# A Mamba and mixture-of-experts block on one core: softplus, D product and gating by quarters, row copies by way of DRAM, and the combine weights in a gate bank

## The chip, the core and the metric

The kernel runs on one core of a Trainium2 chip, as one launch. The metric is the device time of that core in microseconds (us). Engines are named as in the profile: PE is the matrix engine, DVE the vector engine, ACT the scalar (activation) engine, POOL the general engine, SP the queue that issues most DMAs.

## What is computed

Eight sequences of 256 tokens with 256 features pass through three sublayers, each behind a layer norm and a residual: half of a mixture-of-experts FFN, a Mamba mixer with its own MLP, and the same FFN again.

```python
scores = sigmoid(x @ gate_w); topk_w, topk_i = top_k(scores, 6)        # 32 experts
act = silu(x @ wg) * (x @ wu)                                           # 96 wide each
routed = einsum('tef,efd,te->td', act, wd, combine)                     # + shared FFN, 192 wide
# Mamba, 512 channels, 16 states:
z, x, B, C, dt = split(h @ in_proj.T)
dt = softplus(dt @ dt_proj.T + dt_proj_b)
x = silu(causal_conv(x, 4 taps) + conv_b)
h = exp(dt * A) * h + (dt * x) * B           # over 256 time steps, by channel and state
y = sum_n h * C + x * D_param
out = (y * silu(z)) @ out_proj.T
```

## The kernel before

Everything lies with features on partitions and tokens along the free axis. The 512 Mamba channels are four quarters (JC = 4) of 128 partitions. The recurrence of a quarter runs as 8 pairs of states, so there are 32 **units** (UNITS). A unit u is two items: `ub` (PE spreads B into a `side` bank, DVE multiplies it by dt·x, ACT makes the decays) and `unit` (DVE runs the scan over 512 elements, PE spreads C into another `side` bank, DVE multiplies, POOL adds up).

The sequences are software-pipelined over **steps** t = 0 to 9. In step t the first FFN of one sequence, the Mamba mixer of the sequence before it, and the MLP and second FFN of earlier ones run together. Steps 3 to 5 are a hardware loop. In steps 1 and 3 to 7 the two FFN calls share matmuls 512 wide; in steps 2, 8, 9 and 0 they are 256 wide. Mamba is present in steps 1 to 8. Steps 7 and 8 are "own" steps: the second FFN works on the sequence whose MLP ends in the same step, so its routing stands between the MLP and the FFN.

The order of work is planned in Python. `items_of(t)` lists heavy items (MLP chunks `gum`, `down`; FFN chunks `cmb`, `g`, `u`, `down` with the DVE products `by_g`, `by_u` and POOL's `by_comb`) and light items (norms, projections, units, routing `rq`). `merge` spreads the light ones over the heavy ones in proportion to lengths from the tables LENGTH and SHORT. Every engine walks this list in order; DVE and POOL use `late_order`, which holds some items back by a few places.

The projection of a step consists of `split` 0 (B and the dt rank), `split` 1 and 2 (C), `x` 0 and 1 (x with its convolution), `z` 0 and 1, `dt` 0 and 1, `sp` (logarithm on ACT, correction on DVE), `sp_dt` (dt finished), `sp_x` (dt·x), `y0` (x·D). A split writes three bf16 parts into `parts`, which overlays the `decays` buffers; DMAs then copy groups of 32 rows into `bst` and `cst`, and their semaphore is `stacked`. The buffers `ubuf`, `lbuf`, `tmp`, `dtr` and the padded x all overlay `ring`. `yz` multiplies y by silu(z) before the output projection `outp` (L827).

PE has three `gub` banks for `g`, `u` and `gum`, and three `side` banks taken in turn by everything else, `cmb` (L695, the combine weights of three chunks, copied to SBUF by ACT at L862) among them. A bank is waited for through the semaphore of its use three uses ago.

## Time and profile before

| | |
|---|---|
| median of 3 runs | 1869.39 us (1867.44 to 1872.44) |
| the profiled execution | 1871.1 us, its span 1869.3 us |
| PE busy | 1573.3 us (84%) |
| DVE busy | 1300.1 us (70%) |
| POOL, ACT busy | 719.7 us (38%), 696.6 us (37%) |
| mean granted PE clock | 0.940 |

Busy time is the union of an engine's instructions; the rest of the span it is idle. The time of a step is the distance between the FFN ends: about 117, 197, 198, 217, 220, 217, 200, 211, 189 and 99 us for steps 0 to 9.

### The profile page before, as it was taken

To read this page: it belongs to the slowest core of one execution; us is meant where nothing else is said; L and a number is where in the kernel's file an instruction comes from. 1 tells how busy PE (TensorE), PEld (TensorE's weight loads), DVE (VectorE), ACT (ScalarE), POOL (GpSimd) and SP (SyncE) were. 2 spreads that over 40 slices of the span, in tenths; PEclk is the share of its full clock that TensorE was granted. 3 is DMA by queue.
4 is the path that set the end of the run, shared out by engine and by line. 5 is a ranking of instruction groups with operands and counts; after the bars stand their busy time and mean duration, and the time that the engine had idled before them with its cause. 6 is when DMAs were issued, how large, how long until landed. Compare 5 with 4: busy or idle time off the path is not lost. (4 is left out here: it accounts for less than half of the span.)

```text
span 1869.3 us, 23605 instructions
## 1 busy us (share of the span) xinstructions
PE 1573.3 (84%) x7088; PEld 1142.6 (61%) x7088; DVE 1300.1 (70%) x2276; ACT 696.6 (37%) x1384; POOL 719.7 (38%) x814
## 2 busy tenths in 40 slices
PE   6778889776888898898888989889885999757879
PEld 5756556555775556655566555756564666646768
DVE  3435996499747995488946887589945995489633
ACT  3334433444235343444234342453244333433221
POOL 3511554144323552144512553236511663135412
PEclk9979999988899999999999999999997999988989
DMA  7852223232223222222223222332222332223333
GB/s 246 305 176 89 91 68 109 80 114 89 96 81 110 80 80 92 86 94 79 80 79 113 81 78 79 98 110 91 79 78 65 105 102 92 74 93 113 116 101 131
DMA packets 69859, 192.56 MB, mean 103 GB/s; under 512 B 12608, under 2 KB 22048, under 8 KB 69344
## 3 DMA queue, kind: packets, MB, share of 16 engines
q1 hardware_dynamic: 61536, 165.80, 26.4%
q0 software_dynamic: 8192, 25.17, 4.6%
q8 instruction: 63, 1.03, 0.2%
q14 instruction: 68, 0.56, 0.1%
HBM read 165.76 MB, written 15.73 MB: 97 GB/s over the span
## 5 line engine op out<-in xcount | busy, mean ns | idle before, releaser
L641 PE MATMUL gub<-x_hi,wr 128*128 128x512 f32 (+1 forms) x1040 | 428.2, 412 | 58.1 <-DVE hid L1012 38.6
L721 PE MATMUL acc<-hid,w_down 128*128 128x512 f32 (+1 forms) x1040 | 410.1, 521 | 1.1 <-DVE hid L1012 1.1
L1279 POOL TENSOR_TENSOR hid<-hid,weight 128x512 f32<-128x512 f32 (+1 forms) x240 | 263.1, 1097 | 356.9 <-DVE hid L1012 347.1
L873 ACT ACTIVATE hid<-gub 128x256 f32<-128x256 f32 (+1 forms) x324 | 156.1, 483 | 600.2 <-PE gub L643 519.4
L643 PE MATMUL gub<-x_hi,wr 128*128 128x512 f32 (+1 forms) x1040 | 373.6, 359 | 0.0
L642 PE MATMUL gub<-x_lo,wr 128*128 128x512 f32 (+1 forms) x1040 | 373.5, 359 | 0.0
L1292 POOL TENSOR_TENSOR ring<-ring 128x512 f32<-128x512 f32 x192 | 246.8, 1285 | 299.7 <-DVE ring L1176 299.7
L1170 DVE TENSOR_TENSOR_SCAN ring<-decays,side 128x512 f32<-128x512 f32 x256 | 310.0, 1211 | 10.0 <-ACT decays L970 6.6
L641 PEld LDWEIGHTS gub<-x_hi,wr 128*128 128x128 f32 x1040 | 206.6, 199 | 98.8 <-issue 48.0
L721 PEld LDWEIGHTS acc<-hid,w_down 128*128 128x128 f32 x1040 | 190.6, 198 | 96.9 <-issue 82.2
L970 ACT ACTIVATE decays<-dts,a_neg 128x255 f32<-128x255 f32 x512 | 223.0, 497 | 30.7 <-DVE ring L1170 28.7
L643 PEld LDWEIGHTS gub<-x_hi,wr 128*128 128x128 f32 x1040 | 206.4, 198 | 27.5
L642 PEld LDWEIGHTS gub<-x_lo,wr 128*128 128x128 f32 x1040 | 208.2, 200 | 21.1 <-issue 2.9
L1006 DVE SCALAR_TENSOR_TENSOR hid<-hid,gub 128x512 f32<-128x512 f32 (+1 forms) x260 | 149.2, 574 | 100.4 <-ACT hid L873 100.1
L1176 DVE TENSOR_TENSOR ring<-ring,side 128x512 f32<-128x512 f32 x256 | 176.0, 688 | 35.8 <-PE side L817 9.9
L1161 DVE TENSOR_TENSOR side<-dtx,side 128x512 f32<-128x512 f32 x256 | 176.5, 690 | 20.6 <-PE side L814 20.2
L1012 DVE TENSOR_TENSOR hid<-hid,gub 128x512 f32<-128x512 f32 (+1 forms) x260 | 149.3, 574 | 40.0 <-PE gub L643 38.6
L1258 POOL TENSOR_TENSOR pool_pace<-eps_col 128x1 f32<-128x1 f32 x128 | 29.2, 228 | 329.0 <-PE gub L683 191.1
L788 PE MATMUL side<-dts,w_in 128*128 128x256 f32 x448 | 116.3, 411 | 23.6 <-DVE dts L1069 16.9
L814 PE MATMUL side<-bst,sel_b 96*128 96x256 bf16 x512 | 103.9, 286 | 33.1 <-DVE ring L1170 30.7
L817 PE MATMUL side<-cst,sel_c 96*128 96x256 bf16 x512 | 103.8, 286 | 31.8 <-DVE ring L1170 29.5
L683 PE MATMUL gub<-xn_mlp,wm_gu 128*128 128x256 f32 x512 | 119.6, 380 | 1.9 <-DVE xn_mlp L1069 1.6
(117 smaller groups left out, 1668.8 us busy)
## 6 DMA issues: line engine op xcount, KB each, us to landing
wr<-w_halves SPq DMA_DIRECT2D x234, 512.0 KB, 3.2
wm_gu<-in_w_mlp POOLq DMA_DIRECT2D x64, 256.0 KB, 3.0
w_halves<-wr SPq DMA_DIRECT2D x26, 512.0 KB, 5.2
wm_down<-in_w_mlp POOLq DMA_DIRECT2D x64, 128.0 KB, 2.5
w_raw<-in_w_gu SPq DMA_DIRECT2D x26, 256.0 KB, 5.5
cst<-decays SPq DMA_DIRECT2D x192, 32.0 KB, 1.9
xin<-in_x SPq DMA_DIRECT2D x8, 256.0 KB, 3.5
w_in<-in_w_in SPq DMA_DIRECT2D x1, 1792.0 KB, 9.1
```

What stands on the lines that cost most here:

```text
L641: mm(out, w[:, 0, half, k, :], x_hi[:, k, a:b], start=(k == 0), stop=False)
L642: mm(out, w[:, 0, half, k, :], x_lo[:, k, a:b], start=False, stop=False)
L643: last = mm(out, w[:, 1, half, k, :], x_hi[:, k, a:b], start=False, stop=(k == KC - 1))
L721: last = mm(acc[k][:, a:b], w, h[:, a:b], start=(c == 0), stop=(c == (MLP_CHUNKS if mlp else FFN_CHUNKS) - 1))
L873: A(hid[c % HSLOTS][:, a:b], s.gub_of(it)[:, a:b], ACT.Tanh, scale=0.5).then_inc(sem["tanh_done"], 1)
L970: A(decay[u % 2][:, h, 1:SEQ], dts[:, j, 1:SEQ], ACT.Exp, scale=a_neg[:, j, n:n + 1]).then_inc(sem["decay"], 1)
L1012: v.tensor_tensor(h, h, s.gub_of(of)[:, a:b], ALU.mult).then_inc(sem["hidden"], 1)
L1161: v.tensor_tensor(b, twice(dtx[:, j, :]), b, ALU.mult).then_inc(sem["driven"], 1)
L1170: v.tensor_tensor_scan(w.rearrange("p h s -> p (h s)"), decay[u % 2][:, :, :].rearrange("p h s -> p (h s)"), s.side_of(("ub", u))[:, :], 0 ...
L1176: v.tensor_tensor(w, w, pair(s.side_of(it)), ALU.mult).then_inc(sem["read_out"], 1)
L1279: nc.gpsimd.tensor_tensor(h, h, weight[c // 3 % CSLOTS][:, a:b], ALU.mult).then_inc(sem["weighted"], 1)
L1292: add(ysum, ysum, ring[:, u % 3], ALU.add).then_inc(sem["y_sum"], 1)
```

## The change

- `sp_dt`, `sp_x`, `y0` and `yz` work on one quarter at a time. Those of quarter 0 stand before the units; `sp_dt` and `sp_x` of quarter j+1 stand at pair 3 of quarter j, `y0` of quarter j at pair 4, `yz` of quarter j-1 at pair 2 of quarter j. `yz` of the last quarter stays at the end.
- The projection's order becomes split 0, x 0, dt 0, split 1, dt 1, x 1, sp, split 2, z 0, sp_dt 0, sp_x 0, z 1, and the length tables follow.
- `rn`, `ubuf`, `lbuf` and `parts` become buffers of their own. The first column of the decays is zeroed once at the start instead of in every step.
- A split's row copies become one DMA of all parts to DRAM, a wait of the SP queue for it (`spread`), and 3 DMAs back, instead of 12. ACT waits for `spread` before it writes `parts` again; only PE waits for `stacked`, at the first `ub`.
- `cmb` takes a `gub` bank instead of a `side` bank.
- Both FFN products, `by_g` and `by_u`, are on DVE before and after.

```diff
-    project = ([("split", 0), ("x", 0), ("split", 1), ("x", 1), ("z", 0), ("split", 2), ("z", 1),
-                ("dt", 0), ("dt", 1), ("sp",), ("sp_dt",), ("sp_x",), ("y0",)] if mamba else [])
-    units = [(k, u) for u in range(UNITS) for k in ("ub", "unit")] if mamba else []
-    last = [("yz",), ("outp",)] + norm("rms2") if mamba else []
+    project = ([("split", 0), ("x", 0), ("dt", 0), ("split", 1), ("dt", 1), ("x", 1), ("sp",), ("split", 2),
+                ("z", 0), ("sp_dt", 0), ("sp_x", 0), ("z", 1)] if mamba else [])
+    units = unit_items() if mamba else []
+    last = [("yz", JC - 1), ("outp",)] + norm("rms2") if mamba else []
...
+def unit_items():
+    out = []
+    for u in range(UNITS):
+        j, p = u // PAIRS, u % PAIRS
+        out += [("ub", u), ("unit", u)]
+        out += [("yz", j - 1)] if p == 2 and j else []
+        out += [("sp_dt", j + 1), ("sp_x", j + 1)] if p == 3 and j + 1 < JC else []
+        out += [("y0", j)] if p == 4 else []
+    return out
...
-          "dt": 3, "sp": 3, "sp_dt": 3, "sp_x": 2, "y0": 2,
+          "dt": 3, "sp": 4, "sp_dt": 0.6, "sp_x": 0.3, "y0": 0.3,
...
-             "cmb": [("comb_copied", 1)],
              "outp": [("mixed", 2)]},
-    "gub": {"g": [("gated", 1)], "u": [("hidden", 1)], "gum": [("hidden", 1)]},
+    "gub": {"g": [("gated", 1)], "u": [("hidden", 1)], "gum": [("hidden", 1)],
+            "cmb": [("comb_copied", 1)]},
...
-                    for q in range(4):
-                        for a in range(PARTS):
-                            rows = slice(32 * a, 32 * a + 32)
-                            src = parts[32 * q:32 * q + 32, a, :, :]
...
-                            sp.dma_start(dst, src).then_inc(sem["stacked"], 16)
+                    sp.dma_start(rows[i][:, :, hs, :], parts[:, :, hs, :]).then_inc(sem["spread"], 16)
+                    sp.wait_ge(sem["spread"], s.count("spread", it, 16))
+                    for a in range(PARTS):
...
+                        sp.dma_start(dst, src).then_inc(sem["stacked"], 16)
...
                 elif kind == "sp":
-                    dve.wait_ge(sem["stacked"], s.count("stacked", ("split", 2), 16 * 4 * PARTS))
-                    for i in range(2):
-                        v.memset(decay[i][:, :, 0:1], 0.0).then_inc(sem["decay_zero"], 1)
```

DVE's order in the loop step, from its last FFN products ahead of `sp` to the first drive of a unit (`side<-dtx,side`), before. `hid` are the FFN products; `dtx`, `dts` and `xs` hold dt·x, dt and x.

```order
L1131 MEMSET decays 128x2 x2
...
L1136 TENSOR_SCALAR dtx<-ring 128x1024
L1138 TENSOR_TENSOR dtx<-ring,dtx 128x1024
L1142 TENSOR_TENSOR dtx<-dtx,ring 128x1024
L1144 TENSOR_TENSOR dts<-dtx,dts 128x1024
L1012 TENSOR_TENSOR hid<-hid,gub 128x512
L1148 TENSOR_TENSOR dtx<-dts,xs 128x1024
L1006 SCALAR_TENSOR_TENSOR hid<-hid,gub 128x512
L1152 TENSOR_SCALAR xs<-xs,vecs 128x256 x4
L1051 TENSOR_TENSOR res<-x,hn 128x512
L1161 TENSOR_TENSOR side<-dtx,side 128x512
```

The same place now:

```order
L1142 TENSOR_SCALAR dtx<-ubuf 128x1024
L1144 TENSOR_TENSOR dtx<-ubuf,dtx 128x1024
L1016 SCALAR_TENSOR_TENSOR hid<-hid,gub 128x512
L1132 TENSOR_TENSOR ring<-side,parts 128x512
L1135 TENSOR_TENSOR parts<-ring,parts 128x512
...
L1149 TENSOR_TENSOR dtx<-dtx,lbuf 128x256
L1151 TENSOR_TENSOR dts<-dtx,dts 128x256
L1156 TENSOR_TENSOR dtx<-dts,xs 128x256
L1022 TENSOR_TENSOR hid<-hid,gub 128x512
L1096 SCALAR_TENSOR_TENSOR z<-z,side 128x512
L1061 TENSOR_TENSOR res<-x,hn 128x512
L1169 TENSOR_TENSOR side<-dtx,side 128x512
```

The zeroing with its wait has gone, three operations of 1024 elements and the four D products have become three of 256, and the last split stands behind `sp`.

PE's order in a stretch of units of step 2 around a `cmb`, with the semaphore that each waits for, before. `side` and `gub` carry their bank numbers; L814 is `ub`, L817 is `unit`, L641 the first matmul of a `g` or `u`.

```order
L817 MATMUL side2<-cst,sel_c 128x256 [waits scanned]
L695 MATMUL side0<-comb,sel_e 128x256 [waits read_out]
L641 MATMUL gub2<-x_hi,wr2 128x256 [waits hidden,w_back2]
L814 MATMUL side1<-bst,sel_b 128x256 [waits scanned]
L817 MATMUL side2<-cst,sel_c 128x256 [waits read_out]
L641 MATMUL gub0<-x_hi,wr2 128x256 [waits gated]
L814 MATMUL side0<-bst,sel_b 128x256 [waits comb_copied]
L641 MATMUL gub1<-x_hi,wr3 128x256 [waits hidden,w_back3]
```

And now:

```order
L832 MATMUL side2<-cst,sel_c 128x256 [waits scanned]
L710 MATMUL gub2<-comb,sel_e 128x256 [waits hidden]
L656 MATMUL gub0<-x_hi,wr2 128x256 [waits gated,w_back2]
L829 MATMUL side0<-bst,sel_b 128x256 [waits read_out]
L832 MATMUL side1<-cst,sel_c 128x256 [waits scanned]
L656 MATMUL gub1<-x_hi,wr2 128x256 [waits hidden]
L829 MATMUL side2<-bst,sel_b 128x256 [waits read_out]
L656 MATMUL gub2<-x_hi,wr3 128x256 [waits comb_copied,w_back3]
```

The wait of `cmb` has moved from the scan's side to the FFN's, and the `g` and `u` behind it now ask for the product just before them instead of the one before that.

## Rows read from the trace of the kernel before

**Rows 1.** The page, part 1: busy time of each engine.

```profile
PE 1573.3 (84%) x7088; PEld 1142.6 (61%) x7088; DVE 1300.1 (70%) x2276; ACT 696.6 (37%) x1384; POOL 719.7 (38%) x814
```

**Rows 2.** Waits of the whole span: us in total, times, longest.

```profile
PE gub L641 <- DVE hid L1012: 38.6, 18, 9.5
PE side L772 <- DVE c_f L1238: 36.4, 4, 13.6
PE side L695 <- DVE ring L1170: 33.8, 22, 3.6
PE side L827 <- DVE xs L1180: 18.5, 7, 4.0
```

**Rows 3.** Windows, projections: length, busy PE, PEld, DVE, ACT, POOL, clock, DMA share, GB/s.

```profile
136.00:182.00 46.00, 40.91 (x155) 29.73 (x156) 22.41 (x43) 18.97 (x36) 7.00 (x5) 0.96 0.28 91
336.00:381.00 45.00, 31.68 (x148) 26.91 (x149) 24.38 (x51) 18.06 (x38) 7.09 (x17) 0.85 0.28 87
751.00:799.00 48.00, 40.44 (x163) 32.01 (x163) 26.20 (x53) 18.80 (x37) 10.95 (x19) 0.91 0.31 95
1186.00:1231.00 45.00, 41.85 (x166) 33.21 (x166) 23.46 (x47) 19.63 (x38) 9.66 (x19) 0.92 0.33 101
1394.00:1438.00 44.00, 22.67 (x92) 18.19 (x91) 23.53 (x61) 16.34 (x32) 4.77 (x14) 0.74 0.19 52
```

**Rows 4.** Windows of the unit stretches of steps 4, 6 and 7, same columns.

```profile
797.00:929.00 132.00, 119.19 (x495) 74.56 (x493) 119.74 (x187) 50.25 (x103) 67.81 (x57) 0.97 0.25 84
1232.00:1349.00 117.00, 108.15 (x465) 67.96 (x465) 111.99 (x165) 44.37 (x94) 66.58 (x56) 1.00 0.28 93
1434.00:1558.00 124.00, 121.08 (x505) 76.61 (x506) 111.09 (x158) 45.88 (x97) 69.18 (x58) 0.97 0.30 100
```

**Rows 5.** DVE's timeline, `sp` and `y0` in step 4: start, length, idle before.

```profile
790.57 0.07 DVE L1131 MEMSET decays<- 128x2 f32 x2 [4.53 <-DMA cst<-decays]
...
797.36 1.30 DVE L1152 TENSOR_SCALAR xs<-xs,vecs 128x256 f32<-128x256 f32 x3
```

**Rows 6.** PE's timeline in the same stretch of step 4.

```profile
783.06 0.47 PE L641 MATMUL gub<-x_hi,wr 128*128 128x512 f32 x1 [1.60 <-DVE hid L1012]
783.37 0.40 PE L642 MATMUL gub<-x_lo,wr 128*128 128x512 f32 x1
...
795.85 0.77 PE L641 MATMUL gub<-x_hi,wr 128*128 128x512 f32 x1 [4.18 <-DVE hid L1012]
796.42 0.63 PE L642 MATMUL gub<-x_lo,wr 128*128 128x512 f32 x1
```

**Rows 7.** ACT's timeline at split 1 and x 1 of step 4.

```profile
767.25 0.66 ACT L930 ACTIVATE decays<-side 128x256 bf16<-128x256 f32 x2 [4.84 <-DMA bst<-decays]
...
773.16 0.63 ACT L913 ACTIVATE ring<-xs 128x512 f32<-128x512 f32 x1 [3.39 <-DVE xs L1108]
```

**Rows 8.** The SP queue's timeline of step 4: the copies of splits 1 and 2.

```profile
770.04 19.20 SPq L602 DMA_DIRECT2D cst<-decays  x24
```

**Rows 9.** Groups by form: busy us, mean ns of one.

```profile
L998 DVE TENSOR_TENSOR hid<-hid,gub 128x256 f32<-128x256 f32 x64 | 26.9, 420 | 2.2
L1138 DVE TENSOR_TENSOR dtx<-ring,dtx 128x1024 f32<-128x1024 f32 x8 | 9.8, 1225 | 0.3
```

**Rows 10.** Timelines of step 7, DVE and PE, from the MLP's end.

```profile
1408.96 0.76 DVE L1031 SCALAR_TENSOR_TENSOR x<-acc,res 128x256 f32<-128x256 f32 x2 [2.17 <-PE acc L721]
...
1426.21 0.07 DVE L1131 MEMSET decays<- 128x2 f32 x2 [4.85 <-DMA cst<-decays]
...
1436.45 0.45 PE L772 MATMUL side<-ident,c_f 128*96 128x128 bf16 x2 [13.34 <-DVE c_f L1238]
```

**Rows 11.** DMA issues: count, KB each, median us from issue to landing.

```profile
w_halves<-wr SPq DMA_DIRECT2D x26, 512.0 KB, 5.2
cst<-decays SPq DMA_DIRECT2D x192, 32.0 KB, 1.9
out<-x2kept SPq DMA_DIRECT2D x5, 256.0 KB, 2.0
```

More of the change, by code:

```diff
@@ L192 @@
 LENGTH = {"n1": 3, "n2": 3, "nm": 2, "rq": 0.75, "split": 2.25, "x": 10.0, "z": 3,
-          "dt": 3, "sp": 3, "sp_dt": 3, "sp_x": 2, "y0": 2,
-          "ub": 2, "unit": 2, ("unit", UNITS - 1): 8, "rt1": 2,
-          "yz": 3.9, "outp": 3, "g": 1.3, "u": 1.3, "down": 1.7, "gum": 1.7, "cmb": 0.2}
+          "dt": 3, "sp": 4, "sp_dt": 0.6, "sp_x": 0.3, "y0": 0.3,
+          "ub": 2, "unit": 2, ("unit", UNITS - 1): 8, "rt1": 2, "yz": 0.4,
+          ("yz", JC - 1): 3, "outp": 3, "g": 1.3, "u": 1.3, "down": 1.7, "gum": 1.7, "cmb": 0.2}
 SHORT = {"n1": 3, "n2": 6.0, "nm": 2.0, "rq": 0.75, "split": 2.25, "x": 5, "z": 3,
-          "dt": 3, "sp": 3, "sp_dt": 3, "sp_x": 2, "y0": 2,
-          "ub": 2, "unit": 2, ("unit", UNITS - 1): 8, "rt1": 2,
-          "yz": 3.9, "outp": 3, "g": 1.3, "u": 1.3, "down": 1.7, "gum": 1.7, "cmb": 0.2}
+          "dt": 3, "sp": 4, "sp_dt": 0.6, "sp_x": 0.3, "y0": 0.3,
+          "ub": 2, "unit": 2, ("unit", UNITS - 1): 8, "rt1": 2, "yz": 0.4,
+          ("yz", JC - 1): 3, "outp": 3, "g": 1.3, "u": 1.3, "down": 1.7, "gum": 1.7, "cmb": 0.2}
 TAIL = 6
@@ L692, in do @@
                                 pe.wait_ge(sem["comb_ready"], s.count("comb_ready", ("rt2", call), 1))
-                    for over, least in s.last_use("side", it):
+                    for over, least in s.last_use("gub", it):
                         pe.wait_ge(sem[over], least)
-                    mm(s.side_of(it)[:, a:b], sel_e[:, c * P:(c + 1) * P], comb[:, a:b],
+                    mm(s.gub_of(it)[:, a:b], sel_e[:, c * P:(c + 1) * P], comb[:, a:b],
                        start=True, stop=True).then_inc(sem["comb_filled"], 1)
@@ L806, in do @@
                     if kind == "ub" and u == 0:
-                        pe.wait_ge(sem["stacked"], s.count("stacked", ("split", 2), 16 * 4 * PARTS))
+                        pe.wait_ge(sem["stacked"], s.count("stacked", ("split", 2), 16 * PARTS))
                     for over, least in s.last_use("side", it):
@@ L861, in do @@
                         act.wait_ge(sem["weighted"], least)
-                    A(weight[c % CSLOTS][:, a:b], s.side_of(it)[:, a:b], ACT.Copy).then_inc(
+                    A(weight[c % CSLOTS][:, a:b], s.gub_of(it)[:, a:b], ACT.Copy).then_inc(
                         sem["comb_copied"], 1)
@@ L919, in do @@
                         act.wait_ge(sem["y_sum"], least)
-                    if (least := s.count("stacked", it, 0)) is not None:
-                        act.wait_ge(sem["stacked"], least)
+                    if (least := s.count("spread", it, 0)) is not None:
+                        act.wait_ge(sem["spread"], least)
                     b = pair(s.side_of(it))
@@ L951, in do @@
                     act.wait_ge(sem["dt_exp"], s.count("dt_exp", ("dt", 1), 1))
-                    act.wait_ge(sem["x_done"], s.count("x_done", ("x", 1), 1))
-                    act.wait_ge(sem["part_lo"], s.count("part_lo", ("split", 2), 1))
-                    A(lbuf, ubuf, ACT.Ln, bias=1.0).then_inc(sem["dt_ln"], 1)
+                    A(lbuf[:], ubuf[:], ACT.Ln, bias=1.0).then_inc(sem["dt_ln"], 1)
                 elif kind == "ub":
@@ L957, in do @@
                     j, p = u // PAIRS, u % PAIRS
-                    if u == 0:
-                        act.wait_ge(sem["dt_fix"], s.count("dt_fix", ("sp_dt",), 2))
-                        if s.n == 2:
-                            act.wait_ge(a_ready, 1)
-                    if u < 2:
-                        act.wait_ge(sem["stacked"], s.count("stacked", ("split", 2), 16 * 4 * PARTS))
-                        act.wait_ge(sem["decay_zero"], s.count("decay_zero", ("sp",), 2))
+                    if p == 0:
+                        act.wait_ge(sem["dt_fix"], s.count("dt_fix", ("sp_dt", j), 2))
+                    if u == 0 and s.n == 2:
+                        act.wait_ge(a_ready, 1)
                     if (least := s.count("scanned", it, 1, back=2)) is not None:
@@ L982, in _ @@
             v.memset(marks[:, :, 1:2], -2.0).then_inc(zeroed, 1)
-            dve.wait_ge(zeroed, 3)
+            for i in range(2):
+                v.memset(decay[i][:, :, 0:1], 0.0).then_inc(zeroed, 1)
+            dve.wait_ge(zeroed, 5)
             dve.wait_ge(a_exp, 1)
@@ L1156, in do @@
                     j = u // PAIRS
-                    if u == 0:
-                        dve.wait_ge(sem["dtx"], s.count("dtx", ("sp_x",), 1))
+                    if u % PAIRS == 0:
+                        dve.wait_ge(sem["dtx"], s.count("dtx", ("sp_x", j), 1))
                     dve.wait_ge(sem["b_filled"], s.count("b_filled", it, 1))
```

64 lines of the change are left out of this document (34 added, 30 removed).

## The prediction

> **What bounds the kernel now.** I read the busy times first: PE works 84% of the span, DVE 70% [rows 1]. So PE sets the time except where it waits, and the list of waits says for whom. Nearly all of it is DVE [rows 2]: 38.6 us for an FFN product (`hid`), 33.8 us at `cmb` for a scan, 18.5 us at the output projection for `yz`, 36.4 us for the end of routing, most of it in the two own steps. ACT and POOL are free more than half the time.
>
> Then I cut each step into stages by windows. In the projection of a loop step (step 4) PE is busy 40.4 of 48 us and DVE only 26.2 [rows 3]. PE stops there because DVE does things at the wrong moment: DVE stands 4.53 us before a memset that waits for the last row copy [rows 5], then runs the long operations of `sp`, `sp_dt` and `sp_x`, and an FFN product sits behind them; PE waits 4.18 us for it, after 1.60 us earlier in the same stage, and matmuls of one shape last 0.63 us instead of 0.40 for a while behind the long wait [rows 6]. The copies are late because SP issues 24 of them in 19.2 us [rows 8], and ACT stood 4.84 us before split 1 since `parts` was not yet copied out [rows 7]. Step 2 loses the most of the steps with this order (31.7 busy of 45), step 6 the least (41.9 of 45), step 7 over 21 us, since the routing chain is bare there [rows 3, 10].
>
> In the stretch of units both engines are nearly full: DVE 119.7 and PE 119.2 of 132 us in step 4, DVE 112.0 and PE 108.2 of 117 in step 6, and in step 7 PE 121.1 and DVE 111.1 of 124 [rows 4]. This is where the change puts work, and it is the other half of the sum.
>
> **The change part by part.** *First, before the units.* In a loop step 47 us pass from the first projection matmul to the first unit's. The counts of matmuls on the way are those of the planned order: 7 projection groups, 2 `dt`, 2 `gum`, 5 small `down`, 5 `g`, 4 `u`, 1 wide `down`, 35.5 us at the pace of the trace (1.4 us a `g` or `u`, 1.7 a projection group, `gum` or wide `down`, 0.9 a small `down`, 0.7 a `dt`). In the new order one `g` and one `u` fewer stand there (2.8 us, which move into the units), so 32.8 us remain. I then walked PE, ACT and DVE through the new order with the durations of the trace. The wait of DVE at the memset goes, ACT's wait at split 1 shrinks to that for `spread`, and DVE has one short block of 1.9 us (`sp`) and one of 1.3 us in place of 7; so 1.60 and 4.18 us of PE wait go, and with the latter the slow matmuls. New waits come up. Since `cmb` now has a gate bank, the third FFN product of the step needs ACT's copy, and ACT makes it behind the tanh of x 1: the tanh of x 1 itself starts 3.4 us after ACT was free, behind the convolution [rows 7]. By my walk PE is there 2.4 us before the copy ends, and waits 1.3 us more at a later `g`. I take 38.3 us, so the first unit comes **9.0 us earlier**.
>
> The same walk gives 10.9 us for step 2 (13.3 us idle now, 3 us of new wait for the copies, since its FFN matmuls are only half as wide and the copies do not get shorter), 6.9 for step 1 (5.1 us idle now, 2.9 us of FFN moved), and 4.6 for step 6 (3.2 us idle, of which 1.5 goes, 3.1 us moved). In the own steps the chain runs from the MLP's end at 1408.96 to the routing transpose at 1436.45, 27.5 us, and contains DVE's wait of 4.85 us and some 6.7 us of long operations [rows 10]. In the new order x 1 stands ahead of the MLP's end (1.3 us later), `sp` hides under ACT's exponential, and split 2, both z and the first quarter take about 6.8 us: 20.7 us, **5.4 us earlier**. Sum over steps 1 to 8: 6.9 + 10.9 + 3 x 9.0 + 4.6 + 2 x 5.4 = 60.2 us.
>
> *The copies.* Nothing in the trace shows this path whole. From part_lo to the last landing it takes an issue, a landing in DRAM, three issues and a landing. A store of 256 KB lands in 2.0 us, the row copies in 1.9, a store of 512 KB in 5.2 [rows 11]; SP needs 0.6 to 0.8 us an issue of 32 rows [rows 8]. Hence from 2.0 + 1.9 + 2.4 = 6.3 us to 5.2 + 5.2 + 3.2 = 13.6 us; I take 6.5, for 384 KB is nearer to the first. Now it is 7.5 us of issue and 1.9, 9.4 us. Split 2 stands some 10 us of PE work ahead of the first `ub` in a loop step, and its parts need about 4 of them; so at 6.5 us the wait is nearly nothing there and 3 us in step 2, and at 13.6 us it is 7 us in each of six steps.
>
> The Trainium skill (DMA: Bandwidth & Descriptors, section Anatomy of one DMA — SWDGE (gpsimd) path) has a fixed cost of about 2 us for each DMA, mostly the write receipt, and heaviest when the target is HBM. That speaks against a detour which pays it twice in a row. The landing of 2.0 us for the store beside 1.9 us for the copies within SBUF [rows 11] shows no such weight here; if it did, this would be the late-copy rival below.
>
> *Second, in the units.* DVE gets there 5 operations (two of `sp_dt`, `sp_x`, `y0`, `yz`) for each of three quarters and one `y0`, 16 operations of 256 elements at 420 ns [rows 9]: **6.7 us a step**. The price of cutting is in it: 4 x 420 = 1680 ns against 1225 for one of 1024 elements [rows 9], 0.46 us for each of the four. The `y0` of before took 1.30 us for three [rows 5], and stood ahead of the units.
>
> The Trainium skill (VectorE: DVE Perf Modes, section The TRN2 errata — SBUF-src ops pay a fixed extra latency per instruction) advises tiles of 512 elements or more, because many small tiles pay the fixed latency each time. Its table (58 cycles and one an element at 0.96 GHz) would make it 327 ns an operation and 5.2 us a step, an estimate; the trace's 420 ns say 6.7, and I go by the trace.
>
> What of 6.7 us lengthens a step depends on who is full. Where DVE is at its limit all of it counts: steps 1, 2 and 6 (112 of 117 us, and a scan leaves short gaps behind it that nothing else fills), 6.7 each, and nearly all in step 8, 6. In step 7 PE is the limit and DVE has 13 us free: I take 2. In the loop steps both are at 90%; PE gets 2.8 us of FFN more and DVE 6.7: I take 5.8. Sum: 3 x 6.7 + 6 + 2 + 3 x 5.8 = **45.5 us**. The bounds: with DVE's gaps taking it up only PE's moved matmuls count, about 20 us; with every operation in full, 8 x 6.7 + 8 = 62 us.
>
> *Third, the tail.* `yz` at the end falls from 1225 to 420 ns, and PE waits for it in seven of eight steps [rows 2, 9]: 8 x 0.8 = 6.4 us less.
>
> *Fourth, `cmb`.* PE waits 33.8 us in 22 places for a scan there, 1.5 us each [rows 2]. Below: nothing is gained, because PE just waits for the same DVE at the next `ub`. Above: all of it, because PE would have a `g` of 1.4 us to do meanwhile, and DVE some idle time less. DVE is full where these waits are, which is nearer to nothing; I take a quarter, 9 us. ACT's table loads, the buffers made separate and the extra zeroing at the start cost nothing: the number of loads is the same and the zeroing is hidden behind the first loads.
>
> Sum: -60.2 + 45.5 - 6.4 - 9 = -30 us. The profiled execution took 1871.1 us with a span of 1869.3, and the median is 1869.39, so the span and the median may be used alike: 1869.4 - 30 = **1839 us**.
>
> **The rivals.** *Units take little (faster still).* DVE's gaps swallow the quarters, and `cmb` gives back most of its waits, since PE is a `g` further on: -60 + 25 - 6 - 27 = -68, 1801 us. For it speaks the 12 us that each engine is idle in 132 [rows 4]; against it step 6, with DVE at 96%.
>
> *The units give the gain back (same).* Each quarter operation counts in full and `cmb` gives nothing: -60 + 62 - 6 = -4, 1865 us.
>
> *The gate banks are too few (slower).* At a `cmb` the next `g` and `u` wait for the product just before them. DVE runs a scan, a read-out and a drive (2.5 us) between two products, while PE needs 1.4 us for a `g`. Some 50 `cmb` stand among units. If each adds 1.2 us, that is 60 us in place of the 9 gained: -60 + 45 - 6 + 60 = +39, 1908 us. It decides from 0.6 us each. For it speaks that the products are PE's largest wait [rows 2]; against it that these waits lie in the projections, not among the units, with DVE just as full there.
>
> *The copies come late (near the same).* At the upper bound, 7 us in six steps: +42, so 1881 us; at half of that 1860.
>
> **How the numbers follow.** Forecast, 1820 to 1856: 0.5. Faster still, 1795 to 1820: 0.2. Gain given back, 1856 to 1870: 0.14. Gate banks or late copies, above 1870: 0.1; other ways, 0.06. The range 1802 to 1868 holds eight tenths. A measurement of this kernel can tell about 0.3% (5.6 us) from no change. Faster: 0.5 + 0.2 and most of the given-back case, 0.82; same 0.08; slower 0.10.
>
> **What would show it.** Right: no wait of DVE for a DMA before `sp`; the wait of PE for L1012's product down from 38.6 us by half or more; the wait at the routing transpose in steps 7 and 8 about 8 us instead of 13; 12 issues of `cst` and `bst` turned into 4 a split; DVE's busy time up by some 10 us, DVE over 93% in the unit stretch of step 4. Wrong: PE waiting for `cst<-rows` at the first `ub` by more than 3 us; FFN products or ACT's copy of the combine weights as PE's releaser among the units; a unit stretch that grows by more than 9 us in the loop steps.

## The result: slower by half a per cent

| | median of 11 runs | range | ratio to before |
|---|---|---|---|
| before | 1869.39 us | 1863.18 to 1874.38 | |
| changed | 1879.86 us | 1874.44 to 1888.28 | 1.0054 (95%: 1.0035 to 1.0074) |

The forecast was 1839 us (1802 to 1868), with 0.10 for slower. It was wrong in sign, though the change itself is small: 10 us of 1869.

The page of the changed kernel, part 1 (busy time), against [rows 1]:

```profile
PE 1593.2 (85%) x7088; PEld 1150.3 (61%) x7088; DVE 1340.7 (71%) x2358; ACT 699.0 (37%) x1384; POOL 721.6 (38%) x814
```

DVE has 82 instructions more and 40.6 us more of busy time. The forecast had said some 10 us. PE, with the same matmuls, is busy 20 us longer (1593.2 against 1573.3), at a mean granted clock of 0.936 against 0.940, and idle 9.4 us less (286.6 against 296.0). So PE does not wait more in sum than before; its own matmuls take longer. How much of that is the clock is not settled by these rows.

The windows of the changed kernel, same columns as [rows 3, 4]: projections of steps 1, 2, 4, 6 and 7, then the units of steps 4, 6 and 7:

```profile
134.00:182.00 48.00, 39.37 (x143) 28.22 (x143) 23.02 (x42) 19.96 (x37) 6.79 (x5) 0.93 0.30 94
346.00:380.00 34.00, 27.45 (x133) 23.85 (x133) 20.10 (x44) 17.43 (x36) 6.52 (x16) 0.95 0.40 124
754.00:793.00 39.00, 35.67 (x149) 28.74 (x150) 22.76 (x45) 19.85 (x38) 10.21 (x19) 0.96 0.41 127
1183.00:1222.00 39.00, 35.67 (x157) 29.03 (x158) 23.66 (x47) 19.71 (x38) 9.62 (x19) 1.00 0.42 126
1386.00:1436.00 50.00, 33.46 (x133) 27.03 (x133) 24.28 (x67) 20.23 (x37) 6.46 (x18) 0.79 0.25 75
...
793.00:928.00 135.00, 120.54 (x503) 75.07 (x500) 128.79 (x201) 49.12 (x101) 67.65 (x56) 0.97 0.26 87
1222.00:1353.00 131.00, 118.63 (x481) 73.26 (x480) 121.95 (x178) 45.27 (x95) 69.08 (x57) 0.96 0.27 90
1436.00:1564.00 128.00, 124.93 (x517) 78.56 (x516) 118.17 (x164) 45.19 (x97) 72.00 (x60) 0.99 0.31 101
```

The projections became shorter (48 to 39 us in step 4, 45 to 34 in step 2), and the units longer (132 to 135 in step 4, 117 to 131 in step 6, 124 to 128 in step 7), with DVE at 95% in step 4. To add up all eight steps I took the first matmul of each stage from the timelines of both kernels:

| us, summed over steps 1 to 8 | before | changed | difference | forecast |
|---|---|---|---|---|
| projection, to the first `ub` | 377.3 | 339.5 | -37.8 | -60.2 |
| units, to `outp` | 983.9 | 1026.7 | +42.9 | +45.5 and -9 |
| from `outp` to the next projection (the tail) | 255.9 | 262.4 | +6.5 | -6.4 |
| ahead of the first projection, behind the last `outp` | 252.2 | 251.2 | -1.0 | 0 |

The sum is +10.5 us (of unrounded numbers), as the spans say (1879.8 against 1869.3).

Waits of the whole span of the changed kernel, against [rows 2]:

```profile
PE side L832 <- DVE ring L1178: 52.5, 52, 3.6
PE gub L656 <- DVE hid L1016: 44.3, 37, 3.8
...
PE gub L656 <- DVE hid L1022: 23.8, 31, 4.5
...
PE side L787 <- DVE c_f L1247: 19.7, 4, 5.4
PE gub L656 <- ACT weight L877: 17.8, 7, 6.9
PE side L842 <- DVE xs L1189: 17.6, 6, 3.3
...
PE side L754 <- DVE x L1041: 12.6, 3, 5.9
```

The long waits for products (9.5 us) are gone, the wait at the routing transpose has fallen from 36.4 to 19.7 us, and no `cmb` stands for a scan. Against that, PE waits longer at `unit` for the scan (52.5 us), for FFN products in more but shorter pieces (44.3 and 23.8 us in 68 places), for ACT's copy of the combine weights, and in three places for the MLP's end.

**Where DVE's 40.6 us are.** The groups by form of the changed kernel: line, operation, count | busy us, mean ns of one | idle before. L1149 and L1151 are `sp_dt`, L1156 is `sp_x`, L1160 `y0`, L1189 `yz`; L1144 belongs to `sp` and works on all four quarters. The last row gives shortest, median and longest of L1151.

```profile
L1151 DVE TENSOR_TENSOR dts<-dtx,dts 128x256 f32<-128x256 f32 x32 | 36.6, 1145 | 1.1
L1189 DVE TENSOR_TENSOR xs<-xs,z 128x256 f32<-128x256 f32 x32 | 20.1, 629 | 6.1 <-POOL xs L1307 6.1
L1160 DVE TENSOR_SCALAR xs<-xs,vecs 128x256 f32<-128x256 f32 x32 | 17.5, 548 | 0.0
L1156 DVE TENSOR_TENSOR dtx<-dts,xs 128x256 f32<-128x256 f32 x32 | 14.9, 465 | 0.7
L1144 DVE TENSOR_TENSOR dtx<-ubuf,dtx 128x1024 f32<-128x1024 f32 x8 | 13.6, 1704 | 0.3
L1149 DVE TENSOR_TENSOR dtx<-dtx,lbuf 128x256 f32<-128x256 f32 x32 | 13.4, 419 | 0.0
...
L1151 DVE TENSOR_TENSOR dts<-dtx,dts x32: 424/1379/1402, 177.8 to 1717.7; 128x256 f32<-128x256 f32 x32
```

The five quarter operations take 102.6 us together. Before, the same work took 53.4 us in larger pieces, so they grew by 49 us; `sp` grew by 4 us, and the zeroing and other small operations fell by 13 us.

L1149 and L1151, both halves of `sp_dt`, do the same amount of the same kind of work, an addition of 256 elements from two tiles in SBUF. One takes 419 ns and the other 1145 on average. The timelines of the changed kernel at one such place show what differs, DVE first:

```profile
807.47 0.69 DVE L1184 TENSOR_TENSOR ring<-ring,side 128x512 f32<-128x512 f32 x1 [0.50 <-PE side L832]
808.07 0.42 DVE L1149 TENSOR_TENSOR dtx<-dtx,lbuf 128x256 f32<-128x256 f32 x1
808.52 1.39 DVE L1151 TENSOR_TENSOR dts<-dtx,dts 128x256 f32<-128x256 f32 x1
809.95 0.42 DVE L1156 TENSOR_TENSOR dtx<-dts,xs 128x256 f32<-128x256 f32 x1
```

and POOL in the same stretch:

```profile
806.04 1.29 POOL L1288 TENSOR_TENSOR hid<-hid,weight 128x512 f32<-128x512 f32 x1
808.31 1.31 POOL L1301 TENSOR_TENSOR ring<-ring 128x512 f32<-128x512 f32 x1 [0.98 <-DVE ring L1184]
```

The read-out of a unit (L1184) releases POOL's addition (L1301), which runs from 808.31 to 809.62. L1149 began before it and keeps its 0.42 us. L1151 begins at 808.52, inside it, and ends at 809.91, 0.29 us after POOL. The change puts `sp_dt` right behind `unit`, so in all 24 places among the units the second operation starts inside POOL's addition, and all 24 take 1.37 to 1.40 us. In the eight places of the first quarter, ahead of the units, it does not, and takes 0.42 or 0.43 us.

The other groups divide the same way, by whether they start inside an operation of POOL. Of `yz`, 8 of 32 do and take 0.93 to 1.49 us; the other 24 take 0.41 to 0.43. Of `sp_x` it is 2, with 0.83 and 1.38 us; of L1144 4 of 8, with 2.18 us for 1.22. `y0` (L1160) reads one tile and a column instead of two tiles and is held too: of 8 that start inside, 7 take 0.89 to 1.37 us and one 0.34; the others take 0.34 to 0.35. Over 0.42 us an operation (0.35 for `y0`, 1.22 for L1144) the excess is 23 us for L1151, 7 for `yz`, 6 for `y0`, 1.5 for `sp_x` and 4 for L1144, some 41 us in all. That this equals the growth of DVE's busy time is chance: by the same prices the cutting added some 12 us, and other operations became shorter. Experiment 5 takes most of the stall out.

The Trainium skill (SBUF — State Buffer, section Who interferes with whom) says that a VectorE instruction with two inputs in SBUF contends with a GpSimd instruction that reads SBUF, and that the one which issued later stands still until the other is done. The trace agrees: 1.39 us beside 0.42, with an end just behind POOL's. It agrees the other way round too: 50 of POOL's operations on 512 elements start inside one of the DVE operations with two tiles listed above, and take 1.30 to 1.46 us, while 187 that start inside a drive, a read-out or an FFN product take 1.26 to 1.30 (the profile's spans on POOL are rough). Those three kinds of operation have one operand in a PSUM bank and are not held: of 256 drives, 95 start inside an operation of POOL, and the longest of all takes 0.70 us.

```profile
L1169 DVE TENSOR_TENSOR side<-dtx,side x256: 672/689/697, 182.2 to 1755.0; 128x512 f32<-128x512 f32 x128
```

The trace of the kernel before had the sign of it. The eight operations of its line 1144 (the second half of `sp_dt`, 1024 elements from two tiles) took 1.22 us each, but for one that started inside POOL's work and took 2.19:

```profile
L1144 DVE TENSOR_TENSOR dts<-dtx,dts x8: 1224/1225/2186, 181.2 to 1641.7; 128x1024 f32<-128x1024 f32 x8
```

### The profile page after: what moved, and what is told of

It is laid out like the page before. It is cut to its first block and busy times, and to the rows that moved or that the text cites. A ratio compares the mean times of both kernels' runs of the same rounds, so it can differ in the third digit from the quotient of the medians.

```text
span 1879.8 us, 23607 instructions
## 1 busy us (share of the span) xinstructions
PE 1593.2 (85%) x7088; PEld 1150.3 (61%) x7088; DVE 1340.7 (71%) x2358; ACT 699.0 (37%) x1384; POOL 721.6 (38%) x814
## 5 line engine op out<-in xcount | busy, mean ns | idle before, releaser
L656 PE MATMUL gub<-x_hi,wr 128*128 128x512 f32 (+1 forms) x1040 | 431.6, 415 | 89.6 <-DVE hid L1016 44.3
L1288 POOL TENSOR_TENSOR hid<-hid,weight 128x512 f32<-128x512 f32 (+1 forms) x240 | 258.0, 1075 | 347.8 <-DVE hid L1022 336.5
L1301 POOL TENSOR_TENSOR ring<-ring 128x512 f32<-128x512 f32 x192 | 251.8, 1312 | 335.4 <-DVE ring L1184 335.4
L1184 DVE TENSOR_TENSOR ring<-ring,side 128x512 f32<-128x512 f32 x256 | 176.1, 688 | 32.2 <-PE side L832 5.9
L832 PE MATMUL side<-cst,sel_c 96*128 96x256 bf16 x512 | 104.1, 286 | 54.6 <-DVE ring L1178 52.5
L803 PE MATMUL side<-rn,w_in 128*128 128x256 f32 x448 | 114.5, 405 | 16.9 <-DVE rn L1079 16.9
L832 PEld LDWEIGHTS side<-cst,sel_c 96*128 96x128 bf16 x512 | 36.8, 101 | 133.4 <-DVE ring L1178 82.9
```

The lines of the kernel that those rows point to most:

```text
L656: mm(out, w[:, 0, half, k, :], x_hi[:, k, a:b], start=(k == 0), stop=False)
L1184: v.tensor_tensor(w, w, pair(s.side_of(it)), ALU.mult).then_inc(sem["read_out"], 1)
L1288: nc.gpsimd.tensor_tensor(h, h, weight[c // 3 % CSLOTS][:, a:b], ALU.mult).then_inc(sem["weighted"], 1)
L1301: add(ysum, ysum, ring[:, u % 3], ALU.add).then_inc(sem["y_sum"], 1)
```

## The experiments

Each ratio is to the kernel before, measured in the same session (medians 1871.44, 1864.92 and 1869.21 us for the three sessions), from 5 or 6 runs of each kernel tried (12 of `a_cmb_side`, 11 of `b_cmb_gub`). Differences between kernels of different sessions are taken from the ratios, at 1869 us for 1; the intervals of two ratios make such a difference uncertain by some 6 us. Sums over stages are from one profiled execution of each kernel.

The theory is that the quarters among the units cost the time, by standing on DVE while POOL works. The rivals are that the smaller pieces cost it by themselves, that the new order of the projection does, that the gate bank does, and that the detour of the copies does.

**1. The three operations and both products whole again.** `a_whole` is the changed kernel with `sp_dt`, `sp_x`, `y0` on 1024 elements ahead of the units and one `yz` at the end, planned with their old lengths.

```diff
-        out += [("yz", j - 1)] if p == 2 and j else []
-        out += [("sp_dt", j + 1), ("sp_x", j + 1)] if p == 3 and j + 1 < JC else []
-        out += [("y0", j)] if p == 4 else []
...
-                    v.tensor_tensor(dts[:, j], dtx[:, j], dts[:, j], ALU.add).then_inc(sem["dt_fix"], 1)
+                    v.tensor_tensor(dts[:], dtx[:], dts[:], ALU.add).then_inc(sem["dt_fix"], 1)
```

> The changed kernel with softplus, D product and gating whole again: sp_dt, sp_x and y0 on 1024 elements ahead of the units, yz on 1024 at the end, lengths of before for them; banks, buffers, copies and the order of the projection stay. Theory 'quarters': DVE's busy time falls by 30 to 40 us from 1341, the unit stretches shrink by 4 us a step, the projections and tails grow by 2 to 3, so 1860 to 1872 us. Theory 'gate bank': it stays at 1880 or gets slower, since only the places of the work changed.

Measured: 1828.13 us, 0.9779 (0.9746 to 0.9813), span 1819.1, 51 us less than the changed kernel. The theory of the quarters had expected only 1860 to 1872. The window of its units in step 4:

```profile
773.00:902.00 129.00, 115.61 (x494) 72.06 (x492) 120.77 (x186) 50.46 (x103) 67.20 (x56) 1.00 0.28 90
```

Summed as above, the units take 960.2 us and the projections 348.8. So in the profiled executions the quarters cost 66.5 us in the units and gave 9.3 back ahead of them; with the tails that is 61 us. The one of `a_whole` was its fastest, 7 us under its median, so the 51 us of the medians are the better price of the whole. The rest of the change is a gain of 2.2%.

**2. The copies within SBUF again.** `a_copies` keeps everything but has 12 copies a split.

```diff
-                    sp.dma_start(rows[i][:, :, hs, :], parts[:, :, hs, :]).then_inc(sem["spread"], 16)
-                    sp.wait_ge(sem["spread"], s.count("spread", it, 16))
+                    for q in range(4):
+                        for a in range(PARTS):
...
+                            sp.dma_start(dst, src).then_inc(sem["stacked"], 16)
```

> The changed kernel with the 12 copies a split inside SBUF again instead of the way by DRAM. If the DRAM way gains (fewer issues, ACT free earlier at splits 1 and 2): slower, 1890 to 1900 us, PE waiting 3 us more at the first ub of each step. If the DRAM way costs: 1875 us or below.

Measured: 1902.82 us, 1.0173 (1.0139 to 1.0207). A little slower than the 1890 to 1900 expected if the detour gains. The detour by way of DRAM is worth 22 us here, so the rival that it costs time falls. With 12 copies PE waits for them at the first `ub` of every step, as the waits of this kernel show:

```profile
PE side L826 <- DMA cst<-parts: 17.7, 8, 5.5
```

**3. The projection's old order.** `a_order`:

```diff
-    project = ([("split", 0), ("x", 0), ("dt", 0), ("split", 1), ("dt", 1), ("x", 1), ("sp",), ("split", 2),
-                ("z", 0), ("sp_dt", 0), ("sp_x", 0), ("z", 1)] if mamba else [])
+    project = ([("split", 0), ("x", 0), ("split", 1), ("x", 1), ("z", 0), ("split", 2), ("z", 1),
+                ("dt", 0), ("dt", 1), ("sp",), ("sp_dt", 0), ("sp_x", 0)] if mamba else [])
```

> The changed kernel with the projection's old order (split 0, x 0, split 1, x 1, z 0, split 2, z 1, dt 0, dt 1, sp, sp_dt 0, sp_x 0). Theory 'x 1 ahead of the MLP's end costs what the order gains' (it delays the norm and routing chain in the own steps): no slower than the changed kernel, 1872 to 1880 us, with steps 7 and 8 shorter by 3 us each. Otherwise, if the new order pays: 1890 us or more, by PE's waits for FFN products at sp.

Measured: 1851.53 us, 0.9896 (0.9866 to 0.9925), so the new order costs 30 us in this kernel, where neither theory expected less than 1872. Summed, the projections take 42.7 us less (296.8) and the units 17.9 more (1044.6). In the own steps the projections fall from 49.5 and 50.9 us to 44.3 and 43.3, in the loop steps from 39.0 to 33.5. PE's wait for the MLP's end falls from 12.6 to 7.4 us and that for ACT's copy from 17.8 to 6.9, while the routing transpose stands little longer (22.4 us for 19.7). Of the 32 us between the spans 16 are idle time of PE, and these two waits make up as much; the other 16 are busy time of PE (1576.8 for 1593.2, granted clock 0.946 for 0.936). DVE's busy time is the same (1341.6 for 1340.7).

**4. `cmb` in a side bank.** `a_cmb_side`:

```diff
+             "cmb": [("comb_copied", 1)],
              "outp": [("mixed", 2)]},
-    "gub": {"g": [("gated", 1)], "u": [("hidden", 1)], "gum": [("hidden", 1)],
-            "cmb": [("comb_copied", 1)]},
+    "gub": {"g": [("gated", 1)], "u": [("hidden", 1)], "gum": [("hidden", 1)]},
```

> The changed kernel with one part undone: cmb takes a side bank again. Theory 'gate bank' (the g and u behind a cmb wait for the FFN product just before them): it gets faster than the changed kernel by 10 us or more, to 1870 or below, and PE's waits for the products of L1016 and L1022 (68 us in the changed kernel) fall to some 40. Rival theory 'quarters' (the quarter operations among the units are what costs): the bank matters little or is a gain, so 1880 to 1890 us, with waits of 30 us or more for a scan back at cmb.

Measured: 1872.05 us, 1.0000 (0.9978 to 1.0021), 0.5% or 10 us less than the changed kernel, between the two outcomes expected. The projections are 11.8 us shorter in sum, the units 6.7 longer and the tails 10.3 shorter. The waits for products fall from 68 to 47 us. The wait for the scan is back, as large as before, and no wait for ACT's copy stands in the list:

```profile
PE side L710 <- DVE ring L1178: 32.8, 22, 2.4
PE gub L656 <- DVE hid L1016: 28.0, 16, 7.7
```

**5. The same quarters, one place earlier on DVE.** `a_gap` leaves the orders of PE, ACT and POOL and every count alone. DVE does the quarters that stand behind a unit between that unit's scan and its read-out, so that they are done when that read-out releases POOL.

```diff
+                    j, p = u // PAIRS, u % PAIRS
+                    if p == 2 and j:
+                        piece(s, ("yz", j - 1))
+                    if p == 3 and j + 1 < JC:
+                        piece(s, ("sp_dt", j + 1))
+                        piece(s, ("sp_x", j + 1))
+                    if p == 4:
+                        piece(s, ("y0", j))
                     dve.wait_ge(sem["c_filled"], s.count("c_filled", it, 1))
                     dve.wait_ge(sem["scanned"], s.count("scanned", it, 1))
                     v.tensor_tensor(w, w, pair(s.side_of(it)), ALU.mult).then_inc(sem["read_out"], 1)
```

> The changed kernel with its quarter operations of the units (sp_dt, sp_x, y0, yz) moved by one place on DVE: between a unit's scan and its read-out instead of behind the read-out, which is what starts POOL's addition. Theory 'shared port' (an operation whose two operands both lie in SBUF stands still while POOL runs its own): the second sp_dt operation falls from a median of 1379 ns to below 500, DVE's busy time by 20 us or more, the time to 1850 to 1865 us. Rival theory 'more work' (it is the number of DVE operations among the units that costs): durations and the time stay, 1875 to 1885 us.

Measured: 1832.04 us, 0.9806 (0.9779 to 0.9833), 46 us less than the changed kernel with the same work, and more than the 1850 to 1865 us that the theory of the shared port expected. Its groups by form, where L1008 is L1151 of the changed kernel, L1015 is L1160, and L1006 is L1149:

```profile
L1006 DVE TENSOR_TENSOR dtx<-dtx,lbuf 128x256 f32<-128x256 f32 x32 | 15.8, 493 | 0.0
...
L1008 DVE TENSOR_TENSOR dts<-dtx,dts 128x256 f32<-128x256 f32 x32 | 13.6, 425 | 1.1
L1015 DVE TENSOR_SCALAR xs<-xs,vecs 128x256 f32<-128x256 f32 x32 | 11.2, 349 | 0.0
```

1145 ns have become 425. The timelines of one place, DVE and then POOL:

```profile
815.02 1.21 DVE L1203 TENSOR_TENSOR_SCAN ring<-decays,side 128x512 f32<-128x512 f32 x1
816.15 0.40 DVE L1006 TENSOR_TENSOR dtx<-dtx,lbuf 128x256 f32<-128x256 f32 x1
816.58 0.42 DVE L1008 TENSOR_TENSOR dts<-dtx,dts 128x256 f32<-128x256 f32 x1
817.04 0.43 DVE L1012 TENSOR_TENSOR dtx<-dts,xs 128x256 f32<-128x256 f32 x1
```

```profile
813.89 1.29 POOL L1321 TENSOR_TENSOR hid<-hid,weight 128x512 f32<-128x512 f32 x1
818.22 1.29 POOL L1334 TENSOR_TENSOR ring<-ring 128x512 f32<-128x512 f32 x1 [3.05 <-DVE ring L1217]
```

POOL's stretch without work, 815.18 to 818.22, covers all three. All 32 operations of L1008 take 424 to 426 ns. The stall is not gone everywhere: 10 of 32 of L1006 take 0.56 to 0.73 us, and 6 `yz` are still long. DVE's busy time falls by 33 us to 1308.0. The quarters now also fill a wait that DVE had ahead of the read-out (0.50 us in the row of L1184 above): its idle time there falls from 32.2 to 19.3 us in sum. These two come to the 46 us, but the edit makes both at once, so the share of each in the time was not told apart. On PE's side, 31 us of the 49 between the spans are idle time and 17.5 are busy time (1575.7, granted clock 0.948).

**6. Quarters, but all ahead of the units.** `a_pre` keeps pieces of 256 elements and their count, and does those of quarters 1 to 3 and all `y0` before the first unit, the four `yz` at the end. The planned lengths are adapted.

```diff
+               + [(k, j) for j in range(1, JC) for k in ("sp_dt", "sp_x")]
+               + [("y0", j) for j in range(JC)] if mamba else [])
-    last = [("yz", JC - 1), ("outp",)] + norm("rms2") if mamba else []
+    last = [("yz", j) for j in range(JC)] + [("outp",)] + norm("rms2") if mamba else []
```

> The changed kernel with all quarter operations kept at 256 elements but out of the units: sp_dt, sp_x and y0 of all quarters ahead of the units, yz of all quarters at the end. Place against size. If the place costs (port or a full DVE): near the kernel with whole operations, 1830 to 1840 us. If the size costs: 1860 us or more.

Measured: 1828.23 us, 0.9798 (0.9772 to 0.9824), the same as `a_whole` (0.9779, 0.9746 to 0.9813). DVE's busy time is 1315.2 us beside 1304.7, so the pieces do take it 10.5 us longer, but nothing of that shows in the time; the place costs what was lost.

**7. `sp_dt` and `sp_x` ahead, `y0` and `yz` among the units.** `a_spre`:

```diff
-        out += [("sp_dt", j + 1), ("sp_x", j + 1)] if p == 3 and j + 1 < JC else []
...
+               + [(k, j) for j in range(1, JC) for k in ("sp_dt", "sp_x")] if mamba else [])
```

> The changed kernel with sp_dt and sp_x of all quarters ahead of the units, y0 and yz by quarters among them. Theory 'shared port': the stretched operation is sp_dt's second (23 of the 36 us by which DVE's busy time is too long), so most of the loss goes with it: 1845 to 1855 us. If every operation among the units costs alike: 9 of 16 are gone from the units, 1850 to 1862 us.

Measured: 1842.43 us, 0.9872 (0.9847 to 0.9897). Between the changed kernel and `a_pre` lie 48 us; `sp_dt` and `sp_x` make 34 of them, `y0` and `yz` 14. That is somewhat less time than either theory expected (1845 us at the least); the larger share falls to the operations that the stall holds most.

**8. Whole operations, old order, side bank.** `w_order_side` is `a_whole` with the edits of 3 and 4 as well, so that of the change only the copies and the separate buffers remain.

```diff
-                ("z", 0), ("sp_dt", 0), ("sp_x", 0), ("z", 1), ("y0", 0)] if mamba else [])
+                ("dt", 0), ("dt", 1), ("sp",), ("sp_dt", 0), ("sp_x", 0), ("y0", 0)] if mamba else [])
...
+             "cmb": [("comb_copied", 1)],
```

> Three parts undone together: whole operations, the projection's old order, and cmb in a side bank; kept are the separate buffers, the zeroing at the start and the copies by way of DRAM. If the three losses add (44, 28 and 8 us): 1800 us. If they overlap, because each only frees the same PE waits: 1815 to 1830 us.

Measured: 1828.37 us, 0.9795 (0.9769 to 0.9822). As expected if the losses overlap. It equals `a_whole` within some 8 us, so the losses of 30 and 10 us from experiments 3 and 4 do not add to that of the quarters: with whole operations, order and bank together cost nothing that shows. Why they cost 40 us beside the quarters was not found.

**9. The copies alone on the kernel before.** `b_copies`:

```diff
-                    for q in range(4):
-                        for a in range(PARTS):
...
+                    sp.dma_start(rows[i][:, :, hs, :], parts[:, :, hs, :]).then_inc(sem["spread"], 16)
+                    sp.wait_ge(sem["spread"], s.count("spread", it, 16))
```

> The kernel before with one part alone: each split's rows by way of DRAM, 4 issues instead of 12 (parts still overlays the decays). The reverse edit in the changed kernel cost 1.2%, 22 us. DVE's wait for the last copy at the memset of sp (4.5 us a step) falls to 1 or 2 us and ACT's at split 1 to nothing; PE's wait for the product behind sp shrinks with them: 1845 to 1855 us. If the gain hangs on the new order: within 5 us of before.

Measured: 1828.28 us, 0.9782 (0.9763 to 0.9801). This one edit gives 41 us, more than the 14 to 24 expected. Its windows of the projection and the units of step 4:

```profile
733.70:772.50 38.80, 36.51 (x161) 29.84 (x162) 24.34 (x47) 18.68 (x36) 10.93 (x19) 1.00 0.46 143
772.50:905.00 132.50, 115.24 (x491) 71.89 (x490) 121.89 (x190) 50.34 (x103) 67.74 (x57) 1.00 0.25 84
```

The projection takes 38.8 us, as short as in the changed kernel, with the old order and with three long operations on DVE. The units stay at 132.5. Summed over the steps the projections lose 37.0 us here and 37.8 with the whole change. DVE's waits for the last copy ahead of `sp`, 30.8 us in seven steps before (4.53 of them in [rows 5]), have become:

```profile
DVE decays L1134 <- DMA cst<-rows: 11.8, 7, 3.5
```

**10. The gate bank alone on the kernel before.** `b_cmb_gub` is the edit of 4 the other way round.

```diff
-             "cmb": [("comb_copied", 1)],
...
+            "cmb": [("comb_copied", 1)]},
```

> The kernel before with one part of the change alone: cmb in a gate bank. Undoing this part in the changed kernel won 0.5%, nearly all of it ahead of the units. If the bank costs wherever it stands: 1875 to 1885 us, with waits of PE for FFN products and for ACT's copy in place of the 34 us for a scan. If it costs only behind the new order, where the copy stands behind the tanh of x 1: no slower than before, 1855 to 1868 us.

Measured: 1862.90 us, 0.9962 (0.9950 to 0.9974). That is 7 us less than before, as expected if the bank costs only behind the new order. The units take 17.3 us less in sum, the projections 5.7 more. The waits that are new:

```profile
PE gub L641 <- DVE hid L1006: 31.4, 30, 3.2
...
PE gub L641 <- ACT weight L862: 12.2, 4, 5.8
```

**11 and 12. Earlier quarters with the old order.** `g_order` is `a_gap` with the edit of 3, `g_order_side` has that of 4 besides.

```diff
+    project = ([("split", 0), ("x", 0), ("split", 1), ("x", 1), ("z", 0), ("split", 2), ("z", 1),
+                ("dt", 0), ("dt", 1), ("sp",), ("sp_dt", 0), ("sp_x", 0)] if mamba else [])
```

> The changed kernel with the quarter operations between scan and read-out, and the projection's old order. The two edits won 2.5% and 1.6% alone. If they add: 1805 us or below. If they overlap, as whole operations did with old order and side bank: 1820 to 1832 us.

> The same with cmb in a side bank as well. If the bank costs 8 us here too: 8 us below the kernel with the old order and the gate bank. If its cost came from standing behind the tanh of x 1, which the old order takes away: no difference beyond 3 us.

Measured: 1813.21 us, 0.9701 (0.9680 to 0.9721), and 1820.65 us, 0.9725 (0.9704 to 0.9746). `g_order` beats both kernels, the one before by 3.0%. It lies between the two outcomes expected: the old order is worth 20 us here, not 30 and not nothing. Its windows of step 4:

```profile
730.00:763.40 33.40, 33.40 (x149) 27.60 (x149) 19.50 (x40) 15.88 (x33) 8.98 (x18) 1.00 0.46 148
763.40:898.30 134.90, 122.42 (x504) 76.39 (x502) 127.74 (x207) 52.77 (x107) 68.69 (x57) 0.96 0.26 87
```

PE has no idle time in this projection at all. With `cmb` in a side bank the median is 7.4 us higher, against both expectations, but the two intervals overlap.

## Why the prediction was wrong

**The step that failed** is the price in "16 operations of 256 elements at 420 ns". The 420 ns came from an FFN product, which reads one operand from a PSUM bank [rows 9]. `sp_dt`, `sp_x` and `yz` read both from SBUF, and the quarters stand right behind the read-out that starts POOL's addition. They take 1145, 629, 548 and 465 ns on average, as shown above, and 49 us more of DVE than the same work before, not 10. Moving them by one place took 46 us off the kernel (experiment 5), which is more than the 41 us by which the forecast missed. The prediction had no term for DVE and POOL holding each other up.

**It was not the only one.** By its terms, the sum of -30 us missed +10.5 by 22.4 us in the projections, 12.9 in the tail and 6.4 in the units. The quarters' own term was too small by 21 us (66.5 for 45.5, of profiled executions), and that is hidden in the units by what follows.

**The units' sum only looks right.** Forecast +36.5 with `cmb` in it, measured +42.9. It is made of other things. With the quarters one place earlier the units take 981.1 us in `a_gap`, 2.8 less than before, even with the FFN work that moved into them; the whole operations leave them at 960.2. So quarters nearly at their own speed cost 21 us of the units' time, where the forecast had 45.5, and with the stall they cost 66.5. That `a_gap` comes to 1832 us, near the forecast of 1839, is no support for the sum: its units come out at -2.8 us for +36.5, and its projections at -36.1 for -60.2. Two errors cancel there.

Of the rivals, that of late copies was nearest by number (1881 us), but its mechanism did not happen. The one in which the units give back the gain (1865 us) was nearest in kind, but from quarters at 420 ns and `cmb` giving nothing, and neither was so.

**The projections gave 37.8 us instead of 60.2**, and for another reason than the walk had. I had credited the new order and the short blocks of DVE with most of it. In experiment 9 the copies alone give 37.0. The parts do not add up, though: the changed kernel without the detour still has projections 16.6 us shorter than before (360.7, experiment 2). The walk's sum also had a gap: 32.8, 2.4 and 1.3 us make 36.5, and it took 38.3 without naming the rest. The length of the detour was right, at 6.5 us forecast. SP's timeline of the changed kernel shows the store of split 1 issued at 769.16, the first copy back at 771.53, and the three issues over at 772.78, and these land in 2.9 us (2.0 for `bst`):

```profile
769.16 0.34 SPq L608 DMA_DIRECT2D rows<-parts  x1
771.53 1.25 SPq L617 DMA_DIRECT2D cst<-rows  x3
...
rows<-parts SPq DMA_DIRECT2D x16, 384.0 KB, 2.3
cst<-rows SPq DMA_DIRECT2D x48, 128.0 KB, 2.9
```

At the first `ub` 5.7 us of wait are left in three places, 3.8 of them in step 2, where 3 were forecast; the rival of late copies, at 7 us in each of six steps, fell. Step by step the forecast was near in steps 2, 4 and 6 (-10.4, -8.2 and -5.6 us beside -10.9, -9.0 and -4.6) and too high by 3 to 4 us in steps 3 and 5 (-5.3 and -6.0 beside -9.0). It failed in step 1 (+2.6 for -6.9) and the own steps (-3.3 and -1.6 for -5.4 each).

**The new order is a loss of 30 us in this kernel, not a gain** (experiment 3). It is a loss of 20 us with the quarters one place earlier, and none that shows with whole operations (experiments 11 and 8), so it is no loss of the order by itself. The order puts x 1 ahead of the MLP's end, and PE stands up to 5.89 us for it; the projections of the own steps are 12.8 us longer than with the old order. The routing transpose itself did what was said: 5.4 us at most for 13.34 [rows 10], better than the 8 forecast.

**The gate bank.** Forecast 9 us of gain, and it was a gain of 7 on the kernel before and a loss of 10 here. Both directions have the same trade, shorter units and longer projections; here the tails are longer too, by 10.3 us. The wait that the walk had put at 2.4 us is there, at 2.12, in the changed kernel's PE timeline of step 4:

```profile
775.63 0.50 PE L656 MATMUL gub<-x_hi,wr 128*128 128x512 f32 x1 [2.12 <-ACT weight L877]
```

ACT makes the copy at 775.00, behind the tanh of x 1 at 774.46, as the walk said. The wait is the same in steps 2 to 6, 2.08 to 2.16 us each. The longest of the seven, 6.9 us, stands in step 0, where there is no Mamba and so no x 1; the kernel before had a wait of 7.8 us for a product in its place. With the old order (experiment 3) two places and 6.9 us in sum are left of the seven and 17.8, as one expects if the tanh of x 1 holds the copy, though the old order moves other work as well. The rival of too few gate banks named waits of 1.2 us for products at some 50 `cmb` among the units; there the bank helps.

**The tail** gained nothing. The last `yz` falls from 1.22 to 0.42 us only in steps 2 to 5. In steps 1 and 6 it rises from 1.21 to 1.47 and 1.49 us, and in steps 7 and 8 it takes 1.49 and 0.93 (2.30 and 1.73 before), held by POOL as above, and PE waits 17.6 us in six places for 18.5 in seven. And `outp` itself became slower: its rows take 44.6 us in the eight steps for 39.4. These are its rows in steps 1 and 5, in PE's timeline of the changed kernel, and the windows over steps 5 and 1:

```profile
306.62 6.74 PE L842 MATMUL side<-xs,w_out 128*128 128x256 f32 x16 [2.64 <-DVE xs L1189]
...
1143.06 6.66 PE L842 MATMUL side<-xs,w_out 128*128 128x256 f32 x16 [3.14 <-DVE xs L1189]
```

```profile
1143.00:1149.00 6.00, 5.94 (x14) 4.78 (x15) 1.20 (x3) 0.00 (x0) 1.27 (x1) 0.50 0.00 0
...
306.60:313.00 6.40, 6.38 (x16) 5.09 (x17) 0.57 (x1) 0.00 (x0) 4.17 (x12) 0.52 0.52 147
```

The granted clock is 0.50 and 0.52, in the main the lower of the two levels (1.2 GHz), behind a stand of 2.6 to 3.1 us. In the kernel before the same 16 matmuls took 3.72 us in step 1 and 5.16 in step 5, so +3.0 and +1.5 us of the tail's +6.5 are the clock. The trace of before has this slow stretch too, in step 4 (6.77 us), and in `a_gap` a stand of 3.29 us in step 4 is followed by 3.72 us at full clock. So its place changes from kernel to kernel, and with it the tail, which is 3.9 us shorter than before in `a_cmb_side`; what decides it stays open.

## What to carry to other kernels

Before an operation with both operands in SBUF is moved on DVE, look at what POOL does in that place: whatever DVE signals just ahead of it may start the POOL operation that then holds it. Take its price from a row with the same kinds of operands, not just the same size. Where the longest of identical operations takes nearly twice the median, look for POOL's work around it. And when a change has several parts, try each alone and together, since here one part gave more than the whole was forecast to give (41 us for 30), the others spent it, and their losses did not add up.
